# Reordering the unit loops of a graph attention kernel: logits one unit ahead, finished rows one unit behind, and an edge pass in another order

## The reference

```python
def _gat(x, src, dst, W, att_src, att_dst, bias, n):      # passes 0 and 1, 4 heads
    xw = (x @ W).reshape(n, H, D)
    a_src = jnp.einsum('nhc,hc->nh', xw, att_src)
    a_dst = jnp.einsum('nhc,hc->nh', xw, att_dst)
    logits = jax.nn.leaky_relu(a_src[src] + a_dst[dst], NEG_SLOPE)
    m = jax.ops.segment_max(logits, dst, num_segments=n)
    ex = jnp.exp(logits - m[dst])
    s = jax.ops.segment_sum(ex, dst, num_segments=n)
    msg = xw[src] * (ex / (s[dst] + EPS))[..., None]
    return jax.ops.segment_sum(msg, dst, num_segments=n).mean(axis=1) + bias
h = relu(_gat(x, ...1) + (x @ lW1 + lb1))
x = layernorm(x + _gat(h, ...2) + (h @ lW2 + lb2))
# pass 2, the edge pass: 64 logits for each edge
att = relu(concat([x[src], x[dst]]) @ W_lin.T + b_lin)
ex = exp(att - segment_max(att, dst)[dst])
new = segment_sum((ex / segment_sum(ex, dst)[dst]) * concat([x[src], x[dst]]), dst)
out = layernorm(x + new @ W_out.T + b_out)
```

## Time and profile before

| | |
|---|---|
| median of 3 runs | 6352.35 us (6350.67 to 6353.27) |
| the profiled execution, its own time | 6352.61 us |
| its span, first to last instruction | 6350.8 us |
| busy: PE, PEld, POOL, DVE, ACT | 5031.8, 4774.7, 4442.4, 3603.0, 2800.2 us |
| granted TensorE clock, mean | 0.635 of full speed |

### The profile page before, as it was taken

How to read it: one execution, slowest core, us unless ns; L and a number is a source line. 1 busy time by engine, 2 the same in 40 slices (tenths; PEclk the granted TensorE clock), 3 DMA queues, 4 the chain that set the end, 5 groups by cost and what they waited for, 6 DMA issues and landing times. The chain is left out here.

```text
span 6350.8 us, 95072 instructions
## 1 busy us (share of the span) xinstructions
PE 5031.8 (79%) x26936; PEld 4774.7 (75%) x26936; DVE 3603.0 (57%) x7809; ACT 2800.2 (44%) x4886; POOL 4442.4 (70%) x4707
## 2 busy tenths in 40 slices
PE   4888888888888688888888888677778787787787
PEld 4777777777777677777777777577777777777776
DVE  4444434334444544444444444388888888888887
ACT  2333323333232455555554545345555555555554
POOL 4777777777775677777777777477766666666662
PEclk6666666666666666666666666655655555556555
DMA  6222222222222222222222222233333233332331
GB/s 146 64 61 64 62 63 64 61 64 61 64 63 48 62 65 68 64 68 64 68 66 66 66 66 66 58 90 93 88 88 86 85 88 86 87 86 85 88 86 45
DMA packets 378756, 462.45 MB, mean 73 GB/s; under 512 B 150006, under 2 KB 258079, under 8 KB 378202
## 3 DMA queue, kind: packets, MB, share of 16 engines
q0 software_dynamic: 150336, 218.46, 15.8%
q1 hardware_dynamic: 227466, 242.43, 13.0%
q10 hardware_dynamic: 864, 0.48, 0.0%
HBM read 425.44 MB, written 39.55 MB: 73 GB/s over the span
## 5 line engine op out<-in xcount | busy, mean ns | idle before, releaser
L975 POOL DMA_INDIRECT rows<-tab,idx_now x4696 | 4439.0, 945 | 1804.2 <-issue 1392.6
L1677 PE MATMUL psum<-own,hot_t 112*128 112x8 f32 x6288 | 1266.3, 342 | 721.9 <-ACT hot_t L1483 681.2
L1677 PEld LDWEIGHTS psum<-own,hot_t 112*128 112x128 f32 x6288 | 1242.8, 305 | 757.1 <-ACT hot_t L1483 477.3
L1710 PE MATMUL psum<-share,rows 128*65 128x52 f32 (+7 forms) x6288 | 1084.8, 357 | 0.3 <-DVE share L1240 0.2
L1526 ACT ACTIVATE turned<-psum 64x112 f32<-64x112 f32 x262 | 67.3, 257 | 2150.6 <-PE psum L1724 2150.6
L1710 PEld LDWEIGHTS psum<-share,rows 128*65 128x65 f32 x6288 | 1003.1, 209 | 4.8 <-DVE share L1240 0.5
L1208 DVE TENSOR_TENSOR_SCAN psum<-cut,psum 48x224 f32<-48x224 bf16 (+1 forms) x393 | 445.6, 1134 | 921.9 <-PE psum L1688 887.4
L1804 PE MATMUL psum<-hot,prob 128*128 128x112 f32 x3144 | 697.8, 419 | 0.0
L1768 PE MATMUL psum<-own,hot_t 112*128 112x64 f32 x3144 | 691.0, 419 | 2.9 <-issue 2.9
L1768 PEld LDWEIGHTS psum<-own,hot_t 112*128 112x128 f32 x3144 | 686.3, 333 | 3.0 <-issue 3.0
L1804 PEld LDWEIGHTS psum<-hot,prob 128*128 128x128 f32 x3144 | 674.2, 328 | 0.0
(11 more groups left out here) (219 smaller groups left out, 6142.7 us busy)
## 6 DMA issues: line engine op xcount, KB each, us to landing
rel_t<-rel_row SPq DMA_DIRECT2D x262, 336.0 KB
rows<-tab,idx_now POOLq DMA_INDIRECT x4696, 2.5
rel_t<-rel_runs SPq DMA_DIRECT2D x131, 336.0 KB
cut<-cut_row SPq DMA_DIRECT2D x524, 60.0 KB
own<-tab SPq DMA_DIRECT2D x262, 63.0 KB
tab<-row SPq DMA_DIRECT2D x131, 112.0 KB
tab<-row SPq DMA_DIRECT2D x131, 63.0 KB
own<-tab SPq DMA_DIRECT2D x131, 56.0 KB
```

The source lines that it names most:

```text
L975: nc.gpsimd.indirect_dma_start(rows_of[p][:, G * c.s + j, :], None, halves[p], bass.IndirectOffsetOnAxis(ap=idx_now[:, c.s, j:j + 1], axis ...
L1677: nc.tensor.matmul(added[:, j, :, :], hot_t[k][:, P * j:P * j + P], own[c.s][:, 0:H].unsqueeze(1).to_broadcast([W, 2, H]), start=j == 0, s ...
L1710: done = nc.tensor.matmul(summed[:, :, LO[j]:HI[j]], rows_g[:, at + j, 0:D + 1], share[:, j, :, 0:SUBS[j]], start=not opened, stop=j == G ...
```

## The change

Passes 0 and 1. (a) `logits(n + 1)` and the exponential of unit c + 1 are issued in iteration c, one unit ahead of the sums, in place of unit c's own; the first unit's stand ahead of the loop. (b) The last part of the finished row (`row_turn`, `extend_row`, `row_rest`) of unit c - 2 is issued in iteration c, in place of that of unit c - 1; the last two units' stand behind the loop. (c) PE's order in an iteration becomes own_part(c+1), extend_row(c-2), fronts(c+1), heads(c-1), mosts(c+1), sums_of(c), turn_row(c-1). ACT copies the sums of unit c - 1 at the head of iteration c and makes `hot_t` of unit c + 2 early in it. DVE's order becomes shares(c), one_hots(c+1), first_most(c+1), row_rest(c-2), row_front(c-1), logits(c+1), row_norm(c-1). (d) `shares` now waits for the sums of the unit before, and `extend_row` for the row block before it, since they share buffers.

Pass 2. (e) `one_hots3(c + 1)` moves ahead of the products of unit c, behind `edge_means(c - 1)`, and its own wait goes: `edge_means` waits for the sums of unit c - 1. (f) `last_row` of unit c - 2 stands behind `turn_ends(c + 2)`, in place of that of unit c - 1 at the end of the iteration. (g) The two transposes of `turn_ends` become one of twice the size. (h) On ACT, `one_hots_turned(c + 2)` moves from the end of the iteration to a place ahead of `relu_over(c + 1)`.

```diff
--- before.py
+++ after.py
@@ -1228,6 +1228,8 @@
                                         ALU.subtract).then_inc(logit_ready, 1)
...
             def shares(n, c):
+                if not (isinstance(n, int) and n == 0):
+                    dve.wait_ge(sums_ready, n)
                 if not c.below(1):
...
                                             None, ALU.mult).then_inc(share_ready, 1)
@@ -1305,20 +1307,22 @@
                     runs_of_edges()
...
                 first_most(p, unit(0))
+                logits(NU * p)
                 for c in units(dve):
                     n = NU * p + c.u
-                    logits(n)
+                    shares(n, c)
+                    if not c.at_least(NU - 1):
+                        one_hots(p, c.plus(1))
+                        first_most(p, c.plus(1))
+                    if not c.below(2):
+                        row_rest(p, c.plus(-2))
                     if not c.below(1):
                         row_front(p, c.plus(-1))
-                    shares(n, c)
                     if not c.at_least(NU - 1):
-                        first_most(p, c.plus(1))
+                        logits(n + 1)
                     if p == 1 and not c.below(1):
                         row_norm(c.plus(-1))
-                    if not c.at_least(NU - 1):
-                        one_hots(p, c.plus(1))
-                    if not c.below(1):
-                        row_rest(p, c.plus(-1))
+                row_rest(p, unit(NU - 2))
                 row_front(p, unit(NU - 1))
...
                     row_norm(unit(NU - 1))
@@ -1347,8 +1351,6 @@
 
...
 
-                if not c.below(1):
-                    dve.wait_ge(sums_ready, 2 * NU + c.u)
                 nc.vector.tensor_tensor(hot3[c.k][:, :, :], of_unit(rel_run, c).unsqueeze(2).to_broadcast([P, G, W]),
...
                     .then_inc(hot_ready, 1)
@@ -1358,12 +1360,11 @@
 
...
                 dve.wait_ge(first_in[c.s], landed(2, c, 1, 1))
-                for k in range(2):
-                    at = G * c.s + (G - 2) * k
-                    nc.vector.transpose(outer[c.s % 3][:, :, 2 * QUAD * k:2 * QUAD * k + 2 * QUAD]
-                                        .rearrange("p j (c b) -> p c j b", b=QUAD),
-                                        rows_e[:, at:at + 2, D:2 * D].rearrange("p c (j a) -> p c j a", a=QUAD))\
-                        .then_inc(ends_turned, 1)
+                at = G * c.s
+                of_two = rows_e[:, at:at + G, D:2 * D].rearrange("p (h t) w -> p h t w", t=2)
+                nc.vector.transpose(outer[c.s % 3][:, :, :].rearrange("p j (c b) -> p c j b", b=QUAD),
+                                    of_two[:, 0:G // 2:G // 2 - 1, :, :])\
+                    .then_inc(ends_turned, 2)
 
...
 
@@ -1409,8 +1410,12 @@
                                                op0=ALU.max, op1=ALU.subtract).then_inc(logit_ready, 1)
...
                     turn_ends(c.plus(2))
+                if not c.below(2):
+                    last_row(c.u - 2, c.plus(-2))
                 if not c.below(1):
                     edge_means(c.u - 1)
+                if not c.at_least(NU - 1):
+                    one_hots3(c.plus(1))
                 dve.wait_ge(prob_ready, n + 1)
...
                 nc.vector.tensor_tensor(prob3[k][:, :, 0:D], middle, rows_e[:, at:at + G, 0:D], ALU.mult)\
@@ -1420,10 +1425,7 @@
                     with_own(c.plus(1))
...
                     last_stats(c.u - 1, c.plus(-1))
-                if not c.at_least(NU - 1):
-                    one_hots3(c.plus(1))
-                if not c.below(1):
-                    last_row(c.u - 1, c.plus(-1))
+            last_row(NU - 2, unit(NU - 2))
             edge_means(NU - 1)
...
             last_row(NU - 1, unit(NU - 1))
@@ -1521,6 +1523,15 @@
                 else:
...
 
+            def raise_logits(p, c):
+                act.wait_ge(logit_ready, NU * p + c.u + 1)
+                nc.scalar.activation(prob[c.k], logit[:, :].rearrange("p (j h) -> p j h", h=H), ACT.Exp)\
+                    .then_inc(prob_ready, 1)
+
+            def keep_sums(p, c):
+                act.wait_ge(sums_ready, NU * p + c.u + 1)
+                nc.scalar.activation(sums[:, :, :], summed, ACT.Copy).then_inc(sums_kept, 1)
+
             def row_turn(p, c):
...
                 nc.scalar.activation(turned[0:D, 0:W], row_t, ACT.Copy).then_inc(row_copied, 1)
@@ -1541,24 +1552,27 @@
                 one_hots_turned(p, unit(0))
...
                 strip_of(p, unit(0))
+                raise_logits(p, unit(0))
                 for c in units(act):
-                    n = NU * p + c.u
+                    if not c.below(1):
+                        keep_sums(p, c.plus(-1))
+                    if not c.below(2):
+                        row_turn(p, c.plus(-2))
                     if not c.at_least(NU - 1):
                         strip_of(p, c.plus(1))
-                    act.wait_ge(logit_ready, n + 1)
-                    nc.scalar.activation(prob[c.k], logit[:, :].rearrange("p (j h) -> p j h", h=H), ACT.Exp)\
-                        .then_inc(prob_ready, 1)
+                    if not c.at_least(NU - 2):
+                        one_hots_turned(p, c.plus(2))
+                    if not c.below(2):
+                        row_rest(p, c.plus(-2))
+                    if not c.at_least(NU - 1):
+                        raise_logits(p, c.plus(1))
                     if not c.at_least(NU - RING):
...
                         row_front(p, c.plus(-1))
-                        row_turn(p, c.plus(-1))
-                    act.wait_ge(sums_ready, n + 1)
-                    nc.scalar.activation(sums[:, :, :], summed, ACT.Copy).then_inc(sums_kept, 1)
-                    if not c.below(1):
-                        row_rest(p, c.plus(-1))
-                    if not c.at_least(NU - 2):
-                        one_hots_turned(p, c.plus(2))
+                keep_sums(p, unit(NU - 1))
+                row_turn(p, unit(NU - 2))
+                row_rest(p, unit(NU - 2))
                 row_front(p, unit(NU - 1))
...
                 row_rest(p, unit(NU - 1))
@@ -1726,6 +1740,9 @@
 
...
                 pe.wait_ge(row_copied, NU * p + c.u + 1)
+                if not (p == 0 and c.below(1)):
+                    pe.wait_ge(row_kept_v, NU * p + c.u)
+                    pe.wait_ge(row_kept_a, NU * p + c.u)
                 if p == 0:
...
                         .then_inc(extra_made, 1)
@@ -1739,18 +1756,20 @@
                 mosts(NU * p)
...
                     n = NU * p + c.u
+                    if not c.at_least(NU - 1):
+                        own_part(p, c.plus(1))
+                    if not c.below(2):
+                        extend_row(p, c.plus(-2))
+                    if not c.at_least(NU - 1):
+                        fronts(p, c.plus(1))
                     if not c.below(1):
...
                     if not c.at_least(NU - 1):
-                        own_part(p, c.plus(1))
-                        fronts(p, c.plus(1))
+                        mosts(n + 1)
                     sums_of(n, c)
...
                         turn_row(p, c.plus(-1))
-                    if not c.at_least(NU - 1):
-                        mosts(n + 1)
-                    if not c.below(1):
-                        extend_row(p, c.plus(-1))
+                extend_row(p, unit(NU - 2))
                 heads(p, NU * p + NU - 1)
```

## The result

The changed kernel takes 6077.7 us (median of 4 runs, 6073.64 to 6078.36), against 6351.51 us for the kernel before beside it. The ratio is 0.9569, with a 95% interval from 0.9552 to 0.9585. The forecast was 6075 us in a range of 6050 to 6145.

The account below looks back on a forecast made before the run. POOL's gathers (14.98 us a unit) bound passes 0 and 1, PE nearly too; a circle of DVE and PE (16.96 us) bound pass 2. Span 6350.8 - 245 (pass 2) - 33 (passes' ends) = 6073, predicted 6075 us, range 6050 to 6145.

Parts of the forecast that it names:

- signs of being wrong: DVE waits in pass 2 at square root or exponential; mean loop gather above 0.944 us; passes 0 or 1 above 1955 us.
- Its own range: Whole time if POOL binds all passes: 6055 to 6095 us, the passes' ends giving 12 more or 20 less.
- The end of pass 2: Pass 2 at POOL's 14.98 us a unit, not 16.96, ends at 6105.6 instead of 6350.8: gain 245 us.
- DVE's circle: Pass 2: without its 2.10 us wait for the sums, DVE alone needs 14.7 us a unit, under POOL's 14.98.
- PE's circle: Passes 0 and 1: 13.3 to 14.5 us a unit in the new order, under POOL's 14.98, so no gain per unit.
- The scans: Passes 0 and 1: two scans between `fronts` and `mosts`, covered only by `heads` (0.99 us), may cost PE 0.3 us.
- The late row: Pass 1: `turn_row` may find its row late, behind `logits(c+1)`, the exponential and a table load; put at 0.5 us.
- The ends of the passes: POOL's stops between passes shrink from 59.5 and 55.66 to 40.5 and 42 us: gain 33 us, bounds 0 and 45.
- Case 2: Pass 2 keeps a wait: half a microsecond beyond what DVE has in hand gives 6141 us, one microsecond 6206; chance 0.22.
- Case 3: The change works in pass 2 alone and passes 0 and 1 keep their ends: 6108 us; chance 0.05.
- Case 4: Slower: DVE without rests disturbs POOL's gathers; decides at 1.307 us each, 6580 us if pass 2 alone stretches; chance 0.03.
- Case 5: Whole kernel: nothing moves, as a replacing wait has the same length as the one removed: 6352 us; chance 0.02.

Follow-up runs that it names:

- e3: Changed kernel with one of the 12 gathers of a unit left out (chunk 5's, units 6 to 129 of each pass): 5696.54 us, ratio 0.8967 to the kernel before.
- e11: Kernel before with edit (e) alone, on a calm chip: 6269.78 us against 6346.29, ratio 0.9879.
- e2: Kernel before with the attention part alone, edits (a) to (d): 6312.42 us, ratio 0.9937.
- e5: Changed kernel with two of the 12 gathers of a unit left out (chunks 5 and 6): 7268.04 us against 8716.71 for the kernel before.
- e8: Changed kernel with one large DVE instruction (128x1344) added to each unit of pass 2: 8277.94 us against 8716.71 for the kernel before.
- e9: Kernel before with edit (e) alone: 8415.92 us against 8617.93 for the kernel before.
- e10: Changed kernel with one large DVE instruction (128x1344) added to each unit of pass 2: 8077.02 us against 8617.93 for the kernel before.
- e7: Changed kernel with one small DVE instruction (128x96) added to each unit of pass 2: 8316.04 us against 8716.71 for the kernel before.
- e12: Changed kernel with one large DVE instruction (128x1344) added to each unit of pass 2, on a calm chip: 6202.91 us against 6346.29, ratio 0.9771.

## Why the prediction was right

Its mechanism held: POOL's gathers set the pace of all three passes, and the gain is that of pass 2 and of the passes' ends. That it came within 3 us is in part luck, since two small misses cancel, as told below. Two of its signs of being wrong came true by a hair, the mean gather in the loops (0.946 us, the line was 0.944) and the length of passes 0 and 1 (1958.7 and 1957.3 us, the line was 1955). Both are the same 0.002 us a gather, some 4 us a pass; the pace is still POOL's. What makes a gather that much longer is open. Its own range of 6055 to 6095 does not follow from the bounds beside it, which give 6063 at the lower end.

**The end of pass 2.** The changed kernel's timeline answers to the earlier trace rows:

```profile
4055.83 0.95 POOL L975 DMA_INDIRECT rows<-tab,idx_now  x1 [40.33 <-DMA tab<-row]
...
4102.08 0.45 DVE L1365 STREAM_TRANSPOSE outer<-rows 128x256 f32<-128x256 f32 x1 [3.11 <-DMA rows<-tab,idx_now]
...
6022.82 0.44 DVE L1365 STREAM_TRANSPOSE outer<-rows 128x256 f32<-128x256 f32 x1
...
6052.81 0.80 ACT L1603 ACTIVATE psum<-logit 128x768 f32<-128x768 f32 x1
```

From unit 2's transpose to unit 130's it is 128 steps of 15.006 us (14.98 forecast), then 30.0 us to the last exponential (29.4 forecast) and 23.2 us to the end (24.2). The pass takes 6076.0 - 4055.8 = 2020 us and not 2262, a gain of 242 us, where 245 was forecast. That POOL and not DVE sets the step is shown by the absence of any wait of POOL, and by e3: less work on POOL makes pass 2 faster, down to DVE's 14.50 us and no further.

**DVE's circle.** Forecast 14.7 us, measured 14.50 in e3. The removed wait stands as forecast; the large transpose takes 445 ns (428 forecast). The timeline of one unit answers to the earlier trace rows:

```profile
5001.38 0.18 DVE L1269 BATCH_NORM_AGGREGATE mean_var<-stat 112x2 f32<-112x6 f32 x1 [0.16 <-DVE stat L1266]
...
5002.13 0.29 ACT L1511 ACTIVATE std<-mean_var,eps 112x1 f32<-112x1 f32 x1
...
5002.98 0.45 DVE L1365 STREAM_TRANSPOSE outer<-rows 128x256 f32<-128x256 f32 x1
5003.35 0.12 DVE L1273 RECIPROCAL inv_std<-std 112x1 f32<-112x1 f32 x1
5003.48 0.46 PE L1803 MATMUL psum<-outer,shifts 128*128 128x96 f32 x2 [1.55 <-DVE outer L1365]
...
5005.23 1.53 DVE L1354 TENSOR_TENSOR hot<-rel_run,psum 128x1344 f32<-128x1344 f32 x1
```

The square root ends at 5002.42 and DVE takes it at 5003.35: 0.9 us in hand, 0.6 forecast. The one-hot starts without a wait. PE waits 1.55 us here and 2.2 on average (269.8 / 120), where I left it 1 us to spare: it is busy for 12.8 us a unit and not 13.4, and its granted clock in pass 2 is 0.58 where it was 0.56.

**Passes 0 and 1.** The unit stays at POOL's pace. PE's circle did not bind: e3 shows it at 13.75 us or less. My bound of 14.5 was too wide on the slow side. The scans cost nothing, where I had put 0.3 us: no wait of PE for them is left in the loops, and `heads`, which covers them, takes 1.72 us there. The late row costs PE 110.7 us in 126 units of pass 1, 0.9 us each where I put 0.5, and it lies inside PE's slack.

**The ends of the passes.** The stops are 32.86 and 40.33 us:

```profile
2057.25 0.95 POOL L975 DMA_INDIRECT rows<-tab,idx_now  x1 [32.86 <-DMA tab<-row]
```

They were forecast at 40.5 and 42. The stops together shrink by 42 us and not 33: the term was short by 9, mostly in pass 0. Against that stands the gather, 1.251 us for 1.248, which in 4696 gathers costs some 12 us, 8 of them in passes 0 and 1. The first gather of pass 2 thus starts 4088.46 - 4055.83 = 32.6 us earlier, where 33 was forecast; two small misses cancel there, by luck.

**The rivals.** Case 2, a wait that stays in pass 2, is excluded by the waits after; e11 shows that it is just what happens when (e) comes without (f) to (h). Case 3 falls with e2: the passes' ends do gain, by 41 us. Case 4, gathers that stretch: 946 ns for 944, far from what decides, with DVE at 92%. The longer gathers at the start of pass 1 are still there, but what sets them off is less plain than the prediction has it: in both kernels the first four gathers of the pass take 0.94 to 0.95 us, and the next eleven 1.24 to 1.31, beside the same alternation of DVE's copies and two-input instructions. They end when that alternation ends, so DVE's part in them is likely; no run tests it.

Case 5 is excluded by the time.

## What to carry to other kernels

A removed wait is worth what the next bound allows. Here the wait was 2.1 us, DVE would have allowed 2.4, and POOL gave 1.9. Before counting on a stall, multiply the count of each engine's work by its pace: POOL, 12 gathers at 1.25 us, was the floor in two passes although it stood idle for a quarter of them, since its gaps were issue and no waits. An experiment that takes a little work from the suspected bound, in both kernels, decides it at once: 0 us before, where another bound stood beside POOL or above it, and 381 us after. A zero alone does not say that the engine is no bound, only that it is not the last one. And when a wait is taken away, see that what stood behind it is in time: the same edit brought 77 us alone and 243 with the moves around it.

## What the runs showed of the hardware

**The same kernel on other chips.** In the jobs of e5 to e8 and of e9 and e10, the kernel before took 8717 and 8618 us, its seven runs on each chip within 0.1%. The other kernels there show that it was not the gathers (945 ns in e7) nor DVE's or ACT's own work (busy for 3584 and 2797 us in e7, for 3570 and 2836 in the changed kernel). In e7's timeline PE stands still between matmuls of one accumulation, with nothing to wait for that the profile shows:

```profile
7001.27 0.34 PE L1826 MATMUL psum<-hot,prob 128*128 128x112 f32 x1 [2.44 <-issue]
7004.07 0.34 PE L1826 MATMUL psum<-hot,prob 128*128 128x112 f32 x1 [2.46 <-issue]
7005.48 0.35 PE L1826 MATMUL psum<-hot,prob 128*128 128x112 f32 x1 [1.06 <-issue]
```

What held PE up is open, and so is whether these stops are the whole of the lost time: the profile puts stops of POOL of up to 10.6 us to issue there, where the changed kernel's are 0.3. In pass 2, where DVE sets the pace, calm units ran as on a calm chip (e8 15.87 to 15.90 us, e12's median 15.90; e9 16.22, e11's median 16.24), so a bunch of intervals can still be read there where a total cannot. In passes 0 and 1 it could not.

**The clock.** PE's mean granted clock in passes 0 and 1 fell from 0.68 and 0.67 to 0.60, though PE does the same work in the same time. What moved is where in the unit PE rests. In pass 0 its rest of 3.2 us now lies ahead of `fronts`, where one of 2.7 us lay ahead of `own_part`. In the unit from 1003 us on, the granted clock is 0.50, the lower level of 1.2 GHz, for the 9 us behind the rest, and 1.00, the level of 2.4 GHz, from 1012 to 1015 us. So the eight matmuls of `heads`, close behind the rest, take 1.72 us in each unit where they took 0.99, while the 24 of `own_part`, now late in PE's busy stretch, take 2.80 us (median) where they took 4.63. In pass 1 PE has two shorter rests, and `own_part` takes 3.78 us there. The change of clock cost nothing, since POOL sets the pace.
